# A linear-attention decoder layer: where the transposes of the key-value sums stand among the projections

## The chip, the cores and the metric

The kernel runs on one core of one Trainium2 chip. The metric is device time in microseconds (us), the median of the runs. An engine takes its own instructions in the order in which they are written; engines meet only through semaphores. PE is TensorE, DVE is VectorE, ACT is ScalarE, POOL is GpSimd, SP issues most of the transfers.

## What is computed

A decoder layer on x of 8 batches x 1024 rows x 512 columns, in three parts, each followed by a layer norm of x plus the part's result:

```
q, k, v = x @ Wq.T + bq, x @ Wk.T + bk, x @ Wv.T + bv     # 16 heads of 32
q', k'  = [cos(p), sin(p)] / sqrt(128),  p = head @ proj / sqrt(32)   # 128 cosines, 128 sines
kv      = sum over the rows of k'^T v      # per batch and head, 256 x 32
x = layernorm(x + (q' kv) @ Wo.T + bo)
x = layernorm(x + rmsnorm(x) @ W_in.T + b_in + row of a decayed context table)
x = layernorm(x + dequant(fp6(x)) @ dequant(fp6(Wf)).T + bias)
```

The change concerns the attention alone: the sums `kv` can be used by the query side only once they are complete, and they have to be transposed on the way.

## The kernel before

**Two stages.** `attention` handles the first line-up (q, k, v, features, kv, output projection, first norm) and writes `normed`; `context_and_quantised` does the other two parts. The first ends at about 1290 us of the span, the second takes the rest. Only the first is changed.

**Batches and chunks.** A batch has two chunks of 512 rows. The engines run batch 0 in mode "first", batches 1 to 7 as one loop body (mode "loop"), and then what is left over as "tail". Work is split into steps, and all engines walk through the same list of steps (lines 112 to 158), each taking its own share of each step. The list is written out by hand in 16 slots, numbered by feature pair w: pairs 0 to 7 are keys, 8 to 15 queries.

**The steps.** K(c, g) and Q(c, g) project chunk c for four heads (group g): 12 matmuls of 512 columns into one PSUM bank, then ACT adds the bias and writes `stack_hi`, and DVE writes the rest, `stack_lo` (line 726), which frees the bank. V(c, t) and W(c, t) (the step "wo") are tiles of 12 matmuls as well: V gives values, W the output projection, which DVE adds to `res` (line 753) and takes statistics of (line 756). phase(w) multiplies by `proj` into four banks of their own; ACT rounds the result (line 610), DVE subtracts (line 713), ACT takes the sine (line 617), DVE the magnitude (line 720), ACT the cosine (line 623). kv(w) adds one key pair into `kv_sum` (32 matmuls, line 530), and out(w) multiplies one query pair by `kv_cols` (16 matmuls, line 556) into the same PSUM, after which ACT and DVE write `att_hi` and `att_lo` (lines 635, 747). W(1, t) within a loop body belongs to the batch before.

**The sums.** save(0) and save(1) ("kvsave", DVE, line 737) copy two groups of `kv_sum` each to `kv_rows`, once kv(5) and kv(7) are done. turned(0) and turned(1) ("kvt") transpose them: PE does four 128x128 transposes into a bank (line 543), DVE copies that to `kv_cols` (line 740). out(8) needs turned(0), out(9) needs turned(1).

**The two banks.** All steps in `GEMM` (K, Q, V, W and kvt) share two PSUM banks in turn, in the order of the list: the n-th takes bank n % 2. Before PE writes one, it waits until DVE has read what the step two places earlier in that list left there:

```
GEMM = ("k", "q", "v", "wo", "kvt")
b = bank[order.ring(mode, s, 2)]
freed(n - 2)        # pe.wait_ge(bank_free, ...)
```

The place of a kvt step in the list thus sets the bank, and the predecessor waited for, of every tile near it. In slots 8 and 9 the list of these steps reads: Q(0,2), turned(0), W(1,1), Q(0,3), turned(1), W(1,2). In mode "first" there are no W(1, t), since they belong to the batch before, and in the tail there is no kvt.

**Beside it.** POOL splits the transposed x of the next chunk into high and low parts (lines 371, 375), one such split once Q(0,3) is done, and computes the norm's factors (lines 397 to 404) once stats(1) in slot 10 is done. Those belong to no slot of the change.

Of the kernel before, what the change touches and what calls it, by code (L numbers as in the profile page):

```python
# [98 lines left out]
def attention_steps():  # L99

    K = lambda c, g: ("k", c, g)
    Q = lambda c, g: ("q", c, g)
    V = lambda c, t: ("v", c, t)
    W = lambda c, t: ("wo", c, t)
    kv = lambda w: ("kv", w)
    out = lambda w: ("out", w)
    sin = lambda w: ("sin", w)
    cos = lambda w: ("cos", w)
    wf = lambda n: ("wf", n)
    save, turned = (lambda n: ("kvsave", n)), (lambda n: ("kvt", n))  # L110
    stats, norm = (lambda c: ("stats", c)), (lambda c, h: ("norm", c, h))
    after = {
        11: [sin(11), Q(1, 1), cos(11), norm(1, 0), norm(1, 1), V(0, 0), out(10)],
        12: [sin(12), Q(1, 2), cos(12), V(0, 1), out(11)],
        13: [sin(13), Q(1, 3), cos(13), W(0, 0), W(0, 1), out(12)],
        14: [sin(14), K(0, 0), cos(14), W(0, 2), W(0, 3), stats(0), out(13)],
        15: [sin(15), K(0, 1), cos(15), V(0, 2), norm(0, 0), out(14), norm(0, 1)],
        0: [sin(0), K(0, 2), cos(0), V(0, 3), out(15)],
        1: [sin(1), K(0, 3), cos(1), V(1, 0), kv(0)],
        2: [sin(2), K(1, 0), cos(2), V(1, 1), kv(1)],  # L120
        3: [sin(3), K(1, 1), cos(3), kv(2)],
        4: [sin(4), K(1, 2), cos(4), V(1, 2), kv(3)],
        5: [sin(5), K(1, 3), cos(5), V(1, 3), kv(4)],
        6: [sin(6), Q(0, 0), cos(6), kv(5)],
        7: [sin(7), Q(0, 1), cos(7), save(0), W(1, 0), kv(6)],
        8: [sin(8), Q(0, 2), cos(8), turned(0), W(1, 1), kv(7), save(1)],
        9: [sin(9), Q(0, 3), turned(1), cos(9), W(1, 2), out(8)],
        10: [sin(10), Q(1, 0), cos(10), W(1, 3), stats(1), out(9)],
    }
    steps = []  # L130
    for w in range(PAIRS_A):
        steps += [("phase", w)] + after[w]
    turn = steps.index(V(0, 0))
    own = {K(0, 0), K(0, 1)} | {V(0, t) for t in range(TPC)}
    left = {x for x in steps[turn:] if x not in own} | {out(15), stats(1)} | {norm(1, h) for h in range(2)} | {W(1, t) for t in range(TPC)}
    steps = steps[turn:] + steps[:turn]

    after = {
        0: [K(0, 1), sin(0), K(0, 2), cos(0), V(0, 0), V(0, 1)],
        1: [sin(1), K(0, 3), cos(1), V(0, 2), V(0, 3), V(1, 0), kv(0)],  # L140
        2: [sin(2), K(1, 0), cos(2), V(1, 1), kv(1)],
    }
    first = [K(0, 0)]
    for w in range(3):
        first += [("phase", w)] + after[w]
    first += [x for x in steps[steps.index(("phase", 3)):] if x not in left]

    after = {
        12: [sin(12), Q(1, 2), wf(0), cos(12), wf(1), out(11)],
        13: [sin(13), Q(1, 3), cos(13), wf(2), W(0, 0), W(0, 1), out(12)],  # L150
        14: [sin(14), cos(14), W(0, 2), W(0, 3), stats(0), out(13)],
        15: [sin(15), cos(15), wf(3), out(14), wf(4), norm(0, 0), norm(0, 1), out(15), wf(5), W(1, 0), W(1, 1), ("ends",), W(1, 2), ("repeats",), W(1, 3),
             stats(1), norm(1, 0), norm(1, 1)],
    }
    tail = [("win",), out(10)]
    for w in range(START + 1, PAIRS_A):
        tail += [("phase", w)] + after[w]
    return steps, left, tail, first


def attention(nc, x, xT, WqT, bq, WkT, bk, WvT, bv, WoT, bo, proj, eye, lens, triangle, WinT, g_res, Wf,
              b_in, g_init, decay, places, ctx_in, kept, normed):

    steps, left, tail, first = attention_steps()
    assert {s for s in steps if s not in left} == set(first)
    GEMM = ("k", "q", "v", "wo", "kvt")
# [1171 lines left out]
```

## Time and profile before

| | us |
|---|---|
| median of 3 runs (1793.45 to 1803.18) | 1795.09 |
| the profiled execution's own time | 1793.82 |
| its span | 1792.0 |
| PE busy | 1635.3 (91%) |
| DVE busy | 1210.9 (68%) |
| ACT busy | 1152.0 (64%) |
| POOL busy | 690.9 (39%) |

Busy times are sums over the span. A row of the timeline gives the start, the duration, the engine, the line, the operation and its tiles, how many such instructions follow one another, and in brackets how long the engine had been idle before it and what ended that. The ends of matmuls are modelled; the starts are not, so distances between starts are what to reckon with. "PEclk" is TensorE's granted clock as a share of 2.4 GHz.

### The profile page before, as it was taken

Reading aid. Unit: us, or ns where it says so; the run is one execution under the profiler, and the core shown is the slowest. Engines: PE = TensorE matmul, PEld = TensorE weight load, DVE = VectorE, ACT = ScalarE, POOL = GpSimd, SP = SyncE. Lnnn points to the kernel's source line nnn. Section 1 sums busy time; section 2 is a strip of 40 time slices with the busy share of each in tenths; the row PEclk is TensorE's granted clock in tenths of the full one; section 3 lists DMA queues with packets and bytes.
Section 4 is the critical chain, followed back from the end, with each engine's and each line's share of the span. In section 5 each row is a group of like instructions: output and inputs, shape, how many; then the busy total and the mean of one; then the engine's idle time right before and its main releaser. Section 6 shows DMA issues by size and latency. Waiting matters only on the chain. (4 is left out here: it accounts for less than half of the span.)

```text
span 1792.0 us, 31892 instructions
## 1 busy us (share of the span) xinstructions
PE 1635.3 (91%) x12212; PEld 1169.2 (65%) x12212; DVE 1210.9 (68%) x1815; ACT 1152.0 (64%) x1510; POOL 690.9 (39%) x641
## 2 busy tenths in 40 slices
PE   4999989998998999999899999987489999999996
PEld 3756766675675666567567656754358777787784
DVE  4577666666765766665676667569767777777774
ACT  2687776776676778667677776766136555565564
POOL 3033105203411420340242044004448777877786
PEclk9999999999999999999999999999789999999998
DMA  4100202200210220120022022001331222222201
GB/s 157 49 21 4 72 1 72 71 1 9 81 54 1 72 72 1 35 88 22 1 72 71 1 72 71 25 1 47 99 104 51 86 77 77 88 70 77 71 36 59
DMA packets 49102, 95.87 MB, mean 54 GB/s; under 512 B 3472, under 2 KB 3792, under 8 KB 48976
## 3 DMA queue, kind: packets, MB, share of 16 engines
q1 hardware_dynamic: 38864, 76.29, 13.6%
q10 hardware_dynamic: 10112, 17.69, 2.7%
q8 instruction: 105, 1.72, 0.4%
q14 instruction: 21, 0.17, 0.0%
HBM read 60.38 MB, written 33.59 MB: 52 GB/s over the span
## 5 line engine op out<-in xcount | busy, mean ns | idle before, releaser
L713 DVE SCALAR_TENSOR_TENSOR feat<-feat,phases 128x1024 f32<-128x1024 f32 x256 | 301.1, 1218 | 209.8 <-ACT feat L610 209.7
L610 ACT ACTIVATE feat<-phases 128x1024 f32<-128x1024 f32 x256 | 248.6, 1024 | 157.7 <-PE phases L469 95.3
L617 ACT ACTIVATE feat<-feat 128x1024 f32<-128x1024 f32 x256 | 272.0, 1063 | 60.6 <-DVE feat L713 52.0
L371 POOL TENSOR_TENSOR xt_hi<-xt_raw,zero 128x512 fp32r<-128x512 f32 x60 | 72.3, 1235 | 534.8 <-PE bank L460 525.9
L623 ACT ACTIVATE feat<-feat 128x1024 f32<-128x1024 f32 x256 | 256.7, 1048 | 12.4 <-DVE feat L720 12.3
L720 DVE TENSOR_SCALAR feat<-feat 128x1024 int32<-128x1024 int32 x256 | 204.0, 799 | 48.2 <-ACT feat L617 47.9
L384 POOL TENSOR_TENSOR res<-res,bo_all 128x512 f32<-128x512 f32 x64 | 78.0, 1243 | 180.0 <-DMA res<-x 179.8
L556 PE MATMUL kv_sum<-feat,kv_cols 128*32 128x512 f32 x1024 | 126.6, 613 | 8.3 <-ACT feat L623 8.3
L530 PE MATMUL kv_sum<-feat,v 128*32 128x256 f32 x2048 | 124.1, 383 | 7.8 <-DVE v L733 7.8
L458 PE MATMUL bank<-xt_hi,win_hi 128*128 128x512 f32 x256 | 109.3, 427 | 19.4 <-POOL xt_lo L375 19.4
L1073 PE MATMUL bank<-wf_hi,back_hi 128*128 128x512 f32 x256 | 109.2, 427 | 3.5 <-DVE back_lo L1211 3.5
L458 PE MATMUL bank<-xt_hi,wq_hi 128*128 128x512 f32 x256 | 107.9, 422 | 3.8 <-DVE stack_lo L726 3.8
L1173 ACT ACTIVATE xs<-xs,shift,rstd 128x512 f32<-128x512 f32 x96 | 71.6, 809 | 60.2 <-POOL shift L1048 60.2
L458 PE MATMUL bank<-wo_hi,att_hi 128*128 128x512 f32 x224 | 97.4, 435 | 13.1 <-DVE stack_lo L726 8.1
L1073 PE MATMUL bank<-win_hi,turn_hi 128*128 128x512 f32 x256 | 104.4, 408 | 2.1 <-DVE turn_lo L1211 2.0
L458 PE MATMUL bank<-wf_hi,xt_hi 128*128 128x512 f32 x256 | 101.3, 396 | 3.7 <-DVE wf_lo L666 2.3
L1075 PE MATMUL bank<-wf_hi,back_lo 128*128 128x512 f32 x256 | 103.9, 406 | 0.0
L1074 PE MATMUL bank<-wf_lo,back_hi 128*128 128x512 f32 x256 | 103.8, 405 | 0.0
L530 PEld LDWEIGHTS kv_sum<-feat,v 128*32 128x32 f32 x2048 | 60.2, 110 | 64.7 <-issue 20.9
L459 PE MATMUL bank<-xt_lo,win_hi 128*128 128x512 f32 x256 | 101.9, 398 | 0.0
L460 PE MATMUL bank<-xt_hi,win_lo 128*128 128x512 f32 x256 | 101.8, 398 | 0.0
L753 DVE TENSOR_TENSOR res<-bank,res 128x512 f32<-128x512 f32 x64 | 43.9, 686 | 85.4 <-PE bank L460 81.3
(196 smaller groups left out, 4088.6 us busy)
## 6 DMA issues: line engine op xcount, KB each, us to landing
normed<-res SPq DMA_DIRECT2D x32, 513.0 KB, 4.5
xt_raw<-xT SPq DMA_DIRECT2D x16, 1024.0 KB, 6.5
res<-x SPq DMA_DIRECT2D x32, 512.0 KB, 4.3
xs<-normed SPq DMA_DIRECT2D x24, 513.0 KB, 4.0
out<-xs ACTq DMA_DIRECT2D x24, 512.0 KB, 2.8
feat<-normed SPq DMA_DIRECT2D x8, 513.0 KB, 3.8
out<-feat ACTq DMA_DIRECT2D x8, 512.0 KB, 2.8
xt_raw<-ctx SPq DMA_DIRECT2D x8, 256.0 KB, 3.7
```

What stands on the lines that cost most here:

```text
L458: pe.matmul(out, left_hi(n), right_hi(n), start=(n == 0), stop=False)
L459: pe.matmul(out, left_hi(n), right_lo(n), start=False, stop=False)
L530: last = pe.matmul(kv_sum[DH * h:DH * h + DH, g, :], v[c][:, t, col:col + DH], feat[2 * (w % 2) + h // 2][:, :, at:at + MAP],  start=(c == ...
L556: last = pe.matmul(b[DH * h:DH * h + DH, :], kv_cols[:, half, g * P + h * DH:g * P + h * DH + DH], feat[2 * (w % 2) + h // 2][:, half, (h ...
L610: act.activation(feat[2 * (w % 2) + p][:, 0, :], phases[:, 2 * p:2 * p + 2, :].rearrange("p h n -> p (h n)"), ACT.Identity, bias=ROUND).th ...
L617: act.activation(f[:, 1, :], f[:, 0, :], ACT.Sin, scale=-TWO_PI).then_inc(sin_done, 1)
L623: act.activation(f[:, 0, :], f[:, 0, :], ACT.Sin, scale=-TWO_PI, bias=HALF_PI).then_inc(feat_ready, 1)
L713: dve.scalar_tensor_tensor(f[:, 0, :], f[:, 0, :], ROUND, phases[:, 2 * p:2 * p + 2, :].rearrange("p h n -> p (h n)"), ALU.subtract, ALU.s ...
L720: dve.tensor_scalar(f[:, 0, :].bitcast(I32), f[:, 0, :].bitcast(I32), MAGNITUDE, None, ALU.bitwise_and).then_inc(fold_ready, 1)
L1073: pe.matmul(o, hi[:, cols], w_hi[:, n, :], start=(n == 0), stop=False)
L1074: pe.matmul(o, hi[:, cols], w_lo[:, n, :], start=False, stop=False)
L1075: last = pe.matmul(o, lo[:, cols], w_hi[:, n, :], start=False, stop=(closed and n == KD - 1))
```

## The change

turned(0) moves in slot 8 from ahead of W(1,1) to behind kv(7), and turned(1) in slot 9 from ahead of cos(9) to behind out(8). Nothing else is edited; banks and waits follow from the list.

```
-        8: [sin(8), Q(0, 2), cos(8), turned(0), W(1, 1), kv(7), save(1)],
-        9: [sin(9), Q(0, 3), turned(1), cos(9), W(1, 2), out(8)],
+        8: [sin(8), Q(0, 2), cos(8), W(1, 1), kv(7), turned(0), save(1)],
+        9: [sin(9), Q(0, 3), cos(9), W(1, 2), out(8), turned(1)],
```

The list of the steps that share the two banks becomes: Q(0,2), W(1,1), turned(0), Q(0,3), W(1,2), turned(1).

## Rows read from the trace of the kernel before

**Rows 1.** The page: busy per engine, and granted clock in 40 slices of the span.
```profile
PE 1635.3 (91%) x12212; PEld 1169.2 (65%) x12212; DVE 1210.9 (68%) x1815; ACT 1152.0 (64%) x1510; POOL 690.9 (39%) x641
...
PEclk9999999999999999999999999999789999999998
```

**Rows 2.** Waits of PE, 0 to 1300 us: total us, times, longest.
```profile
PE bank L458 <- DVE stack_lo L726: 54.4, 33, 3.4
```

**Rows 3.** Timeline of PE, slots 7 to 10 of batch 3.
```profile
551.97 0.39 PE L458 MATMUL bank<-wo_hi,fold 128*128 128x512 f32 x1
...
554.83 1.93 PE L530 MATMUL kv_sum<-feat,v 128*32 128x256 f32 x32
556.69 0.51 PE L476 MATMUL phases<-stack_hi,proj_hi 32*128 32x512 f32 x4
...
557.60 0.50 PE L458 MATMUL bank<-xt_hi,wq_hi 128*128 128x512 f32 x1
...
560.50 0.60 PE L543 MATMUL bank<-ident,kv_rows 128*128 128x128 f32 x4
563.73 0.60 PE L458 MATMUL bank<-wo_hi,fold 128*128 128x512 f32 x1 [2.63 <-DVE stack_lo L726]
...
570.13 0.51 PE L476 MATMUL phases<-stack_hi,proj_hi 32*128 32x512 f32 x4
...
577.93 0.79 PE L458 MATMUL bank<-wo_hi,fold 128*128 128x512 f32 x1 [3.39 <-DVE stack_lo L726]
...
582.31 1.92 PE L556 MATMUL kv_sum<-feat,kv_cols 128*32 128x512 f32 x16
584.16 0.50 PE L476 MATMUL phases<-stack_hi,proj_hi 32*128 32x512 f32 x4
```

**Rows 4.** Stretches of batch 3: busy per engine, then PEclk, DMA share, GB/s.
```profile
552.00:557.00 5.00, 5.00 (x49) 3.28 (x51) 4.53 (x8) 4.59 (x5) 0.00 (x0) 1.00 0.00 0
...
564.00:567.40 3.40, 3.40 (x9) 2.61 (x9) 0.28 (x1) 0.76 (x1) 0.00 (x0) 0.50 0.03 5
```

**Rows 5.** Timeline of PE, batch 0: the longer of its two waits in slots 9 and 10.
```profile
124.91 0.50 PE L458 MATMUL bank<-xt_hi,wq_hi 128*128 128x512 f32 x1 [1.70 <-DVE stack_lo L726]
```

**Rows 6.** Timeline of PE, batch 7: starts of phases 8, 9 and 10.
```profile
1172.08 0.51 PE L476 MATMUL phases<-stack_hi,proj_hi 32*128 32x512 f32 x4
...
1183.96 0.51 PE L476 MATMUL phases<-stack_hi,proj_hi 32*128 32x512 f32 x4
...
1197.41 0.50 PE L476 MATMUL phases<-stack_hi,proj_hi 32*128 32x512 f32 x4
```

**Rows 7.** Timeline of DVE, slots 7 and 8 of batch 3.
```profile
556.20 0.68 DVE L753 TENSOR_TENSOR res<-bank,res 128x512 f32<-128x512 f32 x1
...
562.93 0.74 DVE L726 SCALAR_TENSOR_TENSOR stack_lo<-bank,bq_col,stack_hi 128x512 fp32r<-128x512 f32 x1
563.59 0.68 DVE L740 COPY kv_cols<-bank 128x512 f32<-128x512 f32 x1
...
572.29 2.35 DVE L713 SCALAR_TENSOR_TENSOR feat<-feat,phases 128x1024 f32<-128x1024 f32 x2 [1.33 <-ACT feat L610]
```

**Rows 8.** Timeline of ACT, slots 9 and 10 of batch 3.
```profile
571.23 1.95 ACT L610 ACTIVATE feat<-phases 128x1024 f32<-128x1024 f32 x2 [6.47 <-PE phases L476]
...
576.21 2.10 ACT L623 ACTIVATE feat<-feat 128x1024 f32<-128x1024 f32 x2
```

**Rows 9.** Timeline of POOL, batch 3: the split, then the norm's factors.
```profile
574.18 4.93 POOL L371 TENSOR_TENSOR xt_hi<-xt_raw,zero 128x512 fp32r<-128x512 f32 x4 [70.46 <-PE bank L460]
579.19 5.00 POOL L375 TENSOR_TENSOR xt_lo<-xt_raw,xt_hi 128x512 fp32r<-128x512 f32 x4
```

**Rows 10.** Timeline of DVE, batch 0: two magnitudes beside POOL's split.
```profile
129.07 3.40 DVE L720 TENSOR_SCALAR feat<-feat 128x1024 int32<-128x1024 int32 x2
```

**Rows 11.** Timeline and stretch, PE at slot 13 of batch 2.
```profile
463.62 0.50 PE L458 MATMUL bank<-wo_hi,att_hi 128*128 128x512 f32 x1 [1.42 <-DVE stack_lo L726]
...
463.60:467.00 3.40, 3.38 (x16) 2.33 (x20) 1.57 (x3) 0.40 (x1) 3.32 (x4) 1.00 0.00 0
```

## The prediction, made before the changed kernel was run

> **What bounds the kernel now.** I read the page first: TensorE is busy for 1635.3 of 1792.0 us, far ahead of DVE, ACT and POOL, and its clock is nearly full everywhere [rows 1]. So the questions are where TensorE stands still and where it runs slowly. The view of its waits answers the first for the attention stage (0 to 1300 us): 54.4 us in 33 waits all have one form, a projection tile whose bank waits for DVE's `stack_lo`; the longest is 3.4 us [rows 2].
>
> The timeline of one batch shows where they lie [rows 3]. In slot 8 the transposes start at 560.50 and are modelled to end at 561.10; then TensorE is idle for 2.63 us, and W(1,1) starts at 563.73. In slot 9 the idle time ahead of W(1,2) is 3.39 us. These two make 6.02 us a batch. The cause can be read from the list of bank users: W(1,1) stands two places behind Q(0,2), so it waits until ACT and DVE have read Q(0,2)'s bank. DVE's `stack_lo` runs from 562.93 to 563.67 [rows 7], and W(1,1) starts 0.06 us after it. Between Q(0,2) and W(1,1) TensorE has only 0.60 us of transposes. ACT and DVE are no faster because they are still busy with the sine and the magnitude of pair 8, which their queues hold ahead of it.
>
> There is a second cost behind the idle time. From 564.00 to 567.40 the granted clock is 0.50, that is 1.2 GHz, against 1.00 (2.4 GHz) in the stretch before [rows 4]. W(1,1) then takes far longer than its like: W(1,0), at full clock, goes from 551.97 to the next start at 554.83, 2.86 us. In total, phase 8 to phase 9 is 570.13 - 556.69 = 13.44 us, and phase 9 to phase 10 is 584.16 - 570.13 = 14.03 us [rows 3].
>
> **What the moves do.** No instruction is added or taken away: 4 transposes and one DVE copy per kvt, twice a batch, stand elsewhere. No DMA and no ACT instruction belongs to them, and no step of SP's or POOL's is passed.
>
> *Slot 8.* W(1,1) now stands two places behind W(1,0), whose bank DVE reads from 556.20 to 556.88 [rows 7]. Q(0,2) ends its issue at 560.50, so W(1,1) need not wait. The slot is then a plain sum of starts: phase 557.60 - 556.69 = 0.91, Q 560.50 - 557.60 = 2.90, W 2.86, kv(7) like kv(6) 556.69 - 554.83 = 1.86, transposes 0.60 (the modelled length of four; a bit long). Sum 9.13 us. Gain 13.44 - 9.13 = 4.31 us: 2.63 idle and the rest clock.
>
> *turned(0) itself.* It now waits for Q(0,2)'s `stack_lo`, the wait that W(1,1) had. It comes to its turn at 556.69 + 9.13 - 0.60 = 565.22, and `stack_lo` is there at 563.67: 1.55 us spare, because W(1,1) and kv(7), 4.72 us, now lie between.
>
> *Slot 9.* Phase 9 starts at 565.82 instead of 570.13. Q(0,3) needs the bank of W(1,1), whose issue ended at 563.36. DVE reads it right behind `stack_lo`, some 0.7 us, so by about 564.4; Q(0,3) starts at 566.73. W(1,2) needs turned(0)'s bank: its copy, 0.68 us [rows 7], follows the transposes and is over by 566.6, and W(1,2) starts at 569.63. The slot is 0.91 + 2.90 + 2.86 + out(8) 584.16 - 582.31 = 1.85 + 0.60 = 9.12 us, a gain of 14.03 - 9.12 = 4.91 us. turned(1) waits for Q(0,3)'s `stack_lo`. The rounding of pair 8 would start at about 566.9 (phase start plus 571.23 - 570.13 = 1.10 [rows 3, 8]). From there a chain of ACT and DVE leads to `stack_lo`, which in slot 9 must end before its cosines do, about 578.31 - 571.23 = 7.1 us later [rows 8]; turned(1) comes up at about 574.3. So at worst, with 574.0, it just fits. This is the tightest place. out(8) needs turned(0)'s copy (566.6, against 572.5): covered. Slot 10's W(1,3) needs turned(1)'s copy, due about 576.4 against 578.6: covered. out(9) comes still later.
>
> *What is queued behind the moved steps.* On DVE save(1) stands behind turned(0)'s copy, and the subtraction of phase 9 behind both. Subtractions begin 572.29 - 571.23 = 1.06 us after ACT's rounding begins [rows 7, 8], here about 568.0; copy and save, 1.4 us, end by about 567.3. In slot 10 the copy of turned(1) stands behind out(8)'s `att_lo` and ahead of the subtraction of phase 10. I see a free space of about 0.6 us for its 0.68, and take nothing. Bounds for the DVE side per batch: 0, or both copies in full, 2 x 0.68 = 1.4 us. Near nothing is the better value, since ACT stands still for 6.47 us ahead of its rounding now [rows 8], and after the change its chain of 7.1 us still has to fit only a slot of 9.1.
>
> *POOL.* Its split starts with Q(0,3)'s end, so it moves ahead by the 4.3 us of slot 8, while slot 10's work moves ahead by 9.2. It lasts from 574.18 to 584.19 [rows 9] and now reaches into slot 10, where before it ended ahead of that slot's rounding. Rows of batch 0 show what such an overlap can cost: two magnitudes took 3.40 us beside the split [rows 10]. Slot 10 has room for it. I take 0; the bounds are 0 and 1 us a batch. The Trainium skill, "SBUF — State Buffer", section "Who interferes with whom", says the same in general: VectorE and GpSimd share one port pair, and whoever comes first blocks the other for a whole instruction. That rule alone would give a price for each magnitude and would not change the sum here, as long as the slot is TensorE's.
>
> *The clock.* If the idle time goes, does the clock stay up? Batch 0 has a wait of 1.70 us in slot 10 [rows 5] and batch 2 one of 1.42 us in slot 13, and behind the latter the stretch reads 1.00 [rows 11]. What would be left in slots 8 and 9 is nothing. I take the full clock.
>
> **The sum.** Batches 1 to 6 have the pattern of batch 3: 6 x (4.31 + 4.91) = 55.3 us. In batch 7 the distances are 1183.96 - 1172.08 = 11.88 (the clock stayed up in its slot 8) and 1197.41 - 1183.96 = 13.45 [rows 6]: 2.75 + 4.33 = 7.1 us. Batch 0 has no W(1, t): its bank users follow in the same order as before, Q(0,2), turned(0), Q(0,3), turned(1), so its waits stay, and a copy ahead of phase 10's subtraction could cost up to 0.7. I take 0. The second stage starts earlier and is otherwise the same; a clock step that falls elsewhere may be worth 1 or 2 us either way (one such half-rate stretch cost at most 4.91 - 3.39 = 1.5 us here). Total 62.4 us. The profiled execution took 1793.82 us, so 1731.4; the median of the runs is 1.27 us above it, so about 1732 to 1733. I say 1732. Its own range is 1726 to 1742, from the bounds above (8 batches x 1.0 to 1.4 us on the late side; transposes whose modelled 0.60 is too long, 14 of them, and the clock steps on the early side).
>
> **Rivals.**
>
> *Half a gain: the clock goes on falling.* For it: the price of the slow stretches is a third of my sum. The mechanism would be that the small waits left in each batch, 1.42 us at slot 13 being one, pull the clock down instead. Then only the idle time comes back: 6 x 6.02 and, if batch 7's two waits are each like slot 8's 2.63, 5.3 more = 41.4 us, 1754 us. Against it: the stretch behind that very wait ran at 1.00 [rows 11]. In the Trainium skill, "TensorE: Matmul & The Clock Gate", section "A second HAM failure mode: psum-queue depth-cycling", frequent short idle times between groups that take turns in PSUM banks are said to make the clock oscillate. By that rule this rival would come true, since the two banks still take turns; the trace so far speaks against it. Chance 0.07.
>
> *Half a gain: turned(1) is late.* If Q(0,3)'s `stack_lo` is put off by one more magnitude beside POOL's split (half of 3.40 = 1.7 us [rows 10]) from the 574.0 above, TensorE waits 1.4 us for it, and 7 batches lose 10 us: 1742. This lies in the range, and I count it with the forecast.
>
> *No change: the wait only moves.* TensorE would wait as long ahead of Q(0,3) for DVE's reading of W(1,1), or in turned(0). For it: all of this still hangs on the same DVE queue. Against it: the spare times above, 1.5 and 2.3 us in slot 8. Time 1795. Chance 0.03.
>
> *Slower: DVE's queue becomes the bound.* In slots 8 and 9 the copies now stand directly ahead of the next pair's subtraction, on which sine, magnitude and cosine hang. If that chain set the slots, the stalls would stay, in new places, and 2 x 0.68 us a batch would come on top: 8 x 1.4 = 11 us, 1806. It decides from the point at which the chain of 7.1 us plus a copy is longer than TensorE's slot of 9.1. The rows say 7.8. Chance 0.04.
>
> The forecast gets 0.86. The range for 8 times in 10 is 1725 to 1743. What a measurement can tell from no change is about 0.5%, 9 us: faster 0.93, same 0.03, slower 0.04.
>
> **What would show it.** In the trace after: the projection tiles of slots 8 and 9 without an idle time; the total of the `stack_lo` waits down from 54.4 to about 13 us; phases 8, 9 and 10 each 9.1 us apart; no granted clock of 0.50 between batch 1 and batch 7's slot 9. I am wrong if TensorE shows a wait ahead of turned(0), Q(0,3) or turned(1) of over 1 us, if half-rate stretches appear elsewhere in the batch, or if slot 10 grows beyond the sum of its starts, 0.91 + 2.90 + 2.86 + 1.85 = 8.5 us, which would be the DVE queue or POOL.

## The result and the profile after

The changed kernel takes 1734.43 us (1732.11 to 1734.57, 4 runs) against 1796.76 us (1793.45 to 1803.18, 4 runs) for the kernel before: ratio 0.9645, 95% interval 0.9627 to 0.9664. The forecast was 1732, range 1725 to 1743. The profiled execution took 1734.53 us, with a span of 1732.7.

The page of the changed kernel, busy times and granted clock in 40 slices, against [rows 1]:

```profile
PE 1616.4 (93%) x12212; PEld 1158.9 (67%) x12212; DVE 1212.9 (70%) x1815; ACT 1150.7 (66%) x1510; POOL 689.0 (40%) x641
...
PEclk9999999999999999999999999997799999999998
```

The same instructions run; TensorE is busy for 19 us less: the stretches with a granted clock of 0.50 add up to 90 us of the span instead of 128, and half of those 38 us is 19. The other 40 us of the difference in span are idle time.

The waits of PE, 0 to 1300 us, against [rows 2]; the columns are total us, times, longest:

```profile
PE bank L458 <- DVE stack_lo L726: 16.1, 19, 2.3
```

54.4 us in 33 waits became 16.1 in 19: the 14 waits ahead of W(1,1) and W(1,2) are gone, and one new size stands out, 2.3 us in slot 0 of batch 0, ahead of any step that was moved.

Slots 8, 9 and 10 of batch 3 in the timeline of PE, against [rows 3], and the stretch around them, against [rows 4]:

```profile
541.16 0.51 PE L476 MATMUL phases<-stack_hi,proj_hi 32*128 32x512 f32 x4
...
550.27 0.51 PE L476 MATMUL phases<-stack_hi,proj_hi 32*128 32x512 f32 x4
...
558.78 0.66 PE L543 MATMUL bank<-ident,kv_rows 128*128 128x128 f32 x4
559.36 0.51 PE L476 MATMUL phases<-stack_hi,proj_hi 32*128 32x512 f32 x4
...
567.88 0.51 PE L476 MATMUL phases<-stack_hi,proj_hi 32*128 32x512 f32 x4
```

```profile
541.00:568.00 27.00, 27.00 (x190) 17.54 (x188) 22.64 (x32) 20.51 (x23) 9.99 (x8) 1.00 0.01 1
```

Phases 8, 9, 10 and 11 start 9.11, 9.09 and 8.52 us apart. No row between them carries an idle time, TensorE is busy for 27.00 of 27.00 us, and the granted clock is 1.00 throughout.

DVE in the same slots, against [rows 7]:

```profile
552.42 2.35 DVE L713 SCALAR_TENSOR_TENSOR feat<-feat,phases 128x1024 f32<-128x1024 f32 x2 [0.76 <-ACT feat L610]
554.77 2.57 DVE L720 TENSOR_SCALAR feat<-feat 128x1024 int32<-128x1024 int32 x2
557.27 0.74 DVE L726 SCALAR_TENSOR_TENSOR stack_lo<-bank,bq_col,stack_hi 128x512 fp32r<-128x512 f32 x1
```

The copy of turned(0) (from 550.37) and save(1) (from 550.98, 0.68 us) end 0.76 us before the subtraction of phase 9 can begin. `stack_lo` of Q(0,3) ends at 558.01, and turned(1), which waits for it, starts at 558.78: 0.77 us spare, the tightest place. Beside POOL's split the two magnitudes take 2.57 us, as long as in the kernel before.

Summed over batches 1 to 7 (distances between starts of phases), slots 8 and 9 fell from 190.8 to 127.5 us, a gain of 63.3. Slot 13 grew by 3.1 us and slot 11 by 0.5. Batch 0 took 3.0 us more in its slot 0, ahead of any step that was moved; the executions below show 19.4, 21.0 or 22.4 us there. The sum of any other slot is within 0.9 us of before.

### The profile page after: what moved, and what is told of

It is laid out like the page before. It is cut to its first block and busy times, and to the rows that moved or that the text cites. A ratio compares the mean times of both kernels' runs of the same rounds, so it can differ in the third digit from the quotient of the medians.

```text
span 1732.7 us, 31892 instructions
## 1 busy us (share of the span) xinstructions
PE 1616.4 (93%) x12212; PEld 1158.9 (67%) x12212; DVE 1212.9 (70%) x1815; ACT 1150.7 (66%) x1510; POOL 689.0 (40%) x641
## 5 line engine op out<-in xcount | busy, mean ns | idle before, releaser
L623 ACT ACTIVATE feat<-feat 128x1024 f32<-128x1024 f32 x256 | 256.8, 1047 | 11.2 <-DVE feat L720 11.0
L458 PE MATMUL bank<-wo_hi,att_hi 128*128 128x512 f32 x224 | 90.8, 405 | 13.6 <-DVE stack_lo L726 9.9
L459 PE MATMUL bank<-xt_lo,wq_hi 128*128 128x512 f32 x256 | 101.9, 398 | 0.0
```

Source lines behind the costliest of these rows:

```text
L458: pe.matmul(out, left_hi(n), right_hi(n), start=(n == 0), stop=False)
L459: pe.matmul(out, left_hi(n), right_lo(n), start=False, stop=False)
L623: act.activation(f[:, 0, :], f[:, 0, :], ACT.Sin, scale=-TWO_PI, bias=HALF_PI).then_inc(feat_ready, 1)
```

## The experiments

The times of the kernel before are the medians of its runs beside each group: 1798.54 us for the first four, 1801.45 us for the next four, and a single run of 1798.68 us for the last. The changed kernel was timed beside 1796.76 us, so kernels of different groups are compared by their ratios as well.

**One move alone, slot 8.**

```
-        8: [..., cos(8), turned(0), W(1, 1), kv(7), save(1)],
+        8: [..., cos(8), W(1, 1), kv(7), turned(0), save(1)],
```

> Only turned(0) is moved behind kv(7); slot 9 keeps turned(1) ahead of W(1,2). Theory (each projection tile waits for the bank left two places earlier, so each move removes its own slot's wait, clock loss included): slot 8 falls from 13.44 to 9.11 us in batches 1 to 6 and from 11.88 to 9.11 in batch 7; slot 9 keeps an idle time of 2.64 us ahead of W(1,2) and comes to 13.44, since the slow W(1,1) no longer lengthens it from 3.39. Sum 6 x (4.33 + 0.7) + 2.8 = 33 us, about 1762. Rival (the clock loss needs both waits close together): slot 9 runs at full clock, 11.9 us, and the gain is 43 us, about 1752.

Measured 1770.22 us, ratio 0.9834 (0.9806 to 0.9862): 28 us by the medians, less than the theory (1762 us) and the rival (1752 us) had. Slot 8 is 9.11 us in all seven batches, as both said. Slot 9 is between 14.15 and 15.17 us in batches 1 to 6, longer than either theory had it; only in batch 7 does it run at full clock (11.86 us). Its row and its stretch in batch 1:

```profile
265.45 0.80 PE L458 MATMUL bank<-wo_hi,fold 128*128 128x512 f32 x1 [3.39 <-DVE stack_lo L726]
```

```profile
264.50:271.00 6.50, 5.55 (x16) 3.94 (x20) 1.49 (x3) 1.33 (x2) 6.42 (x6) 0.50 0.00 0
```

The idle time stays at 3.39 us although W(1,1) ran at full clock, so my reason for the step from 2.64 to 3.39 was wrong (the last experiment takes this up). And the half-rate stretch is twice as long here as in [rows 4], 6.8 us against 3.4; that is so in batches 1, 2, 4 and 5, while in batches 3 and 6 it is 3.4 us. The moves do work one by one. The rival in which the clock falls only if both waits are close together is refuted: one wait alone pulls the clock down.

**One move alone, slot 9.**

```
-        9: [sin(9), Q(0, 3), turned(1), cos(9), W(1, 2), out(8)],
+        9: [sin(9), Q(0, 3), cos(9), W(1, 2), out(8), turned(1)],
```

> Only turned(1) is moved behind out(8); slot 8 keeps turned(0) ahead of W(1,1). Theory: slot 9 falls from 14.1 to 9.10 us in batches 1 to 6 and from 13.45 to 9.10 in batch 7, slot 8 keeps 2.63 us idle and 13.44 us: 6 x 5.0 + 4.35 = 34.5 us, about 1761. The two single moves then sum to about 4 us more than both together. Rival (the clock loss needs both waits close together): slot 8 at 11.9 us, gain 44 us, about 1751.

Measured 1755.99 us, ratio 0.9755 (0.9728 to 0.9782): 43 us by the medians. Slot 9 is 9.1 us in all batches. Slot 8 keeps its idle time everywhere, but is 13.4 us in batches 1, 4, 6 and 7, and 11.9 in batches 2, 3 and 5. In one of the latter:

```profile
406.66 0.50 PE L458 MATMUL bank<-wo_hi,fold 128*128 128x512 f32 x1 [2.65 <-DVE stack_lo L726]
```

```profile
399.00:412.00 13.00, 10.35 (x96) 6.90 (x88) 8.26 (x12) 7.22 (x8) 0.00 (x0) 1.00 0.00 1
```

So the same wait of 2.65 us is followed by half rate in some batches and not in others. What removing a wait of this length is worth is not fixed: 2.8 us (11.87 - 9.11) or 4.3 us (13.44 - 9.11). Neither theory had that, and a time between their two follows from it.

**The idle time filled, nothing moved.**

```
+                        for again in range(5):
                         for half in range(2): ...
                             last = pe.transpose(b[:, to:to + P], ...)
```

> The order of before, but TensorE does each set of four transposes five times over (16 redundant transposes more per kvt), which fills most of the idle time with work; bank waits stand where they stood. Theory (a large part of the gain is the clock that falls behind the idle time): idle ahead of W(1,1) and W(1,2) shrinks to some 0.3 to 0.6 us, W(1,1) still starts at the same moment, but at full clock: slots 8 and 9 come to 11.9 us each instead of 13.44 and 14.1. 6 x (1.56 + 2.25) + 1.6 = 24 us, about 1771, no stretch at half clock in slots 8 and 9. Rival (the slow stretches belong to these slots for another reason, the transposes among them): no gain or slower, 1795 or above.

Measured 1774.43 us, ratio 0.9876 (0.9841 to 0.9912): 24 us by the medians, 22 by the ratio. The row of W(1,2) in batch 3, and a stretch that holds slots 8 and 9:

```profile
569.07 0.51 PE L458 MATMUL bank<-wo_hi,fold 128*128 128x512 f32 x1 [1.65 <-DVE stack_lo L727]
```

```profile
549.00:575.00 26.00, 23.45 (x185) 16.24 (x174) 16.23 (x20) 14.30 (x17) 9.60 (x8) 1.00 0.01 1
```

TensorE does 16 more transposes per kvt and the kernel is faster, because the granted clock stays at 1.00: slot 8 is 11.87 us in every batch instead of 13.44, slot 9 is 12.61 instead of 14.1. W(1,2) starts 4.0 us behind the first transpose in both kernels (0.60 + 3.39 us before, 2.35 + 1.65 here), so nothing but the rate of the work behind it has changed. That is 6 x (1.57 + 1.5) + 1.6 = 20 us of the 63: a third of the change's gain is clock, two thirds idle time. Twenty transposes took 2.35 us, 0.12 each, so the fill was smaller than I had reckoned, and 0.90 us in slot 8 and 1.65 us in slot 9 stayed idle.

**Another predecessor, the same moment.**

```
+        8: [sin(8), turned(0), Q(0, 2), cos(8), W(1, 1), kv(7), save(1)],
+        9: [sin(9), turned(1), Q(0, 3), cos(9), W(1, 2), out(8)],
```

> turned(0) and turned(1) stand behind sin(w) and ahead of Q(0,2) and Q(0,3). W(1,1) and W(1,2) no longer wait for the stack_lo of the projection ahead of them, but for DVE's copy of the transposes, which DVE makes behind the magnitudes, at about the moment at which stack_lo is made today. Theory (what counts is when DVE gets to the read, not whose bank it is): the waits stay at 2.5 to 2.7 us, only their releaser is now the copy; within 5 us of before. Rival (it was the neighbourhood of the projection and its stack_lo alone): the waits are gone and the time is about 1735.

Measured 1799.84 us, ratio 1.0 (0.9976 to 1.0023): no change. The row of W(1,1) in batch 4:

```profile
717.73 0.51 PE L458 MATMUL bank<-wo_hi,fold 128*128 128x512 f32 x1 [2.63 <-DVE kv_cols L740]
```

W(1,1) waits 2.63 us as before, for another instruction in the same place of DVE's queue: the copy runs from 716.99, right behind the second magnitude of pair 8. W(1,2) waits 3.77 us, a little longer than the 3.39 of before. Which step stands two places ahead does not decide it alone; it matters when DVE comes to the read.

**The same, ahead of the sine.**

```
+        8: [turned(0), sin(8), Q(0, 2), cos(8), W(1, 1), kv(7), save(1)],
+        9: [turned(1), sin(9), Q(0, 3), cos(9), W(1, 2), out(8)],
```

> turned(0) and turned(1) stand first behind the phase, ahead of sin(w). DVE's copy then comes ahead of the magnitudes. Theory (when DVE gets to the read decides): the copy follows the second subtraction and ends about 5.1 to 5.8 us behind the phase's start, while W(1,1) comes up 0.91 + 0.53 + 2.90 = 4.3 us behind it: 0.8 to 1.4 us idle remain per slot, no clock loss: slots of 9.9 to 10.5, that is 11 to 19 us above the changed kernel: 1746 to 1754. Rival (any place ahead of W(1,t) costs the full wait): about 1795.

Measured 1745.68 us, ratio 0.9696 (0.9667 to 0.9724). DVE copies ahead of its magnitudes (from 693.53; the magnitudes begin at 694.13), and W(1,1) waits 0.80 us, without half rate behind it:

```profile
694.27 0.50 PE L458 MATMUL bank<-wo_hi,fold 128*128 128x512 f32 x1 [0.80 <-DVE kv_cols L740]
```

Slots 8 and 9 take 9.98 to 9.99 us, 0.88 above those of the change; 14 x 0.88 = 12 us should separate the two kernels; it is 11 us by the medians and 9 by the ratios (0.9696 and 0.9645).

**DVE's copy three times over, on the changed kernel.**

```
+                        for again in range(2):
+                            dve.tensor_copy(kv_cols..., b...).then_inc(copied, 1)
+                            dve.wait_ge(copied, 4 * i + 2 * s[1] + again + 1)
```

> The changed kernel with each DVE copy to kv_cols made three times, one behind the other with a semaphore between (1.5 to 2 us more of DVE per kvt, 16 times). Theory (slots 8 and 9 are TensorE's with spare time on the ACT and DVE chain): the subtractions of pairs 9 and 10 come some 1 us later, the chain of 7.1 us still fits the slot of 9.1; nothing waits longer than 0.5 us: 1734 to 1740. Rival (the DVE queue is next in line): all of it shows, 14 x 1.5 = 21 us or more, 1755.

Measured 1735.32 us, ratio 0.9641 (0.9608 to 0.9674), the same as the change within the intervals. One of PE's waits, 180 to 1150 us:

```profile
PE bank L544 <- DVE stack_lo L727: 1.3, 6, 0.2
```

Slot 9 grows from 9.10 to 9.38 us in batches 1 to 6, and what waits there is turned(1), for 0.2 us: the place named as the tightest. DVE's queue is not the next bound in slot 8, and in slot 9 it is reached only with two more copies.

**out(12) between the two tiles of slot 13, on the changed kernel.**

```
-        13: [sin(13), Q(1, 3), cos(13), W(0, 0), W(0, 1), out(12)],
+        13: [sin(13), Q(1, 3), cos(13), W(0, 0), out(12), W(0, 1)],
```

> The changed kernel with out(12) put between W(0,0) and W(0,1) in slot 13 of the loop, so that 1.9 us of TensorE work lie between Q(1,3) plus W(0,0) and the tile that waits for Q(1,3)'s stack_lo. Theory: the wait of 1.07 to 1.31 us ahead of W(0,1) goes in 7 batches: 7 to 8 us less, about 1727. Rival (the wait comes back behind, in slot 14 or in out(12) that waits for its features): the same as the changed kernel.

Measured 1727.38 us, ratio 0.9594 (0.9569 to 0.9619). Slot 13 comes to 11.48 us in batches 1 to 6, where the changed kernel has 12.6 to 12.9, and to 11.47 in batch 0 (12.62); slots 14 and 15 stay at 11.8 and 8.4. PE's waits, 180 to 1150 us, first a row of the changed kernel, then two of this one:

```profile
PE bank L458 <- DVE stack_lo L726: 8.6, 12, 1.3
```

```profile
PE kv_sum L530 <- DVE v L733: 6.8, 7, 1.0
PE bank L458 <- DVE stack_lo L726: 1.7, 6, 0.3
```

**And V(1,3) ahead of K(1,3).**

```
-        5: [sin(5), K(1, 3), cos(5), V(1, 3), kv(4)],
+        5: [sin(5), V(1, 3), K(1, 3), cos(5), kv(4)],
```

> The changed kernel with out(12) between W(0,0) and W(0,1), and V(1,3) ahead of K(1,3) in slot 5, so that kv(4) no longer waits 0.97 us for DVE's reading of V(1,3). Theory: 7.5 us from slot 13 and 8 x 0.97 = 7.8 us from slot 5: about 1719. Rival (the later key product delays the cosines of pair 5, and slots 6 and 7, which are short on TensorE, wait for ACT): slot 5 gains and slots 6 and 7 give it back, 1727 or more.

Measured 1722.53 us (1717.53 to 1730.62, 6 runs), ratio 0.956 (0.9535 to 0.9584), the lowest median of all versions. The interval of its ratio lies clear of the change's, but not clear of that of the kernel with out(12) alone. Slot 5 is 9.44 us instead of 10.10, slots 6 and 7 stay at 6.35 and 9.12, and among PE's waits from 180 to 1150 us is this row:

```profile
PE kv_sum L530 <- DVE v L733: 2.2, 7, 0.3
```

At most 0.3 us of the wait of 0.97 remains, and 8 x 0.66 = 5 us came back and not the 7.8 of the theory.

**POOL's split behind the norm's factors, on the filler kernel.**

```
-                if mode != "last":
-                    split(i + 1, 0, i, mode)
                 powers(2 * i - 1)
+                if mode != "last":
+                    split(i + 1, 0, i, mode)
```

> The filler kernel (order of before, transposes five times over), with POOL's split of the next chunk put behind powers(2i-1), so that it no longer runs beside slot 9's magnitudes. The question: why slot 9's idle time is 3.39 us in batches 1 to 6 and 2.64 in batch 7. Theory (POOL's split holds up DVE's magnitudes, 2.57 us for two against 1.83): slot 9 falls from 12.61 to 11.87 us in batches 1 to 6 as well. Rival (it comes from the slot ahead, W(1,1) or TensorE's own work): slot 9 stays at 12.61 us. The end may shift by what the later split costs elsewhere; only slot 9 is read.

A single run, on another chip, took 1857.09 us; it is read for slot 9 alone. The rows of W(1,2) and of V(0,0) in batch 3:

```profile
594.14 0.50 PE L458 MATMUL bank<-wo_hi,fold 128*128 128x512 f32 x1 [0.90 <-DVE stack_lo L727]
...
622.65 0.79 PE L458 MATMUL bank<-wf_hi,xt_hi 128*128 128x512 f32 x1 [11.23 <-POOL xt_lo L375]
```

Slot 9 is 11.85 to 11.89 us in batches 1 to 6, and its two magnitudes, which beside the split take 2.57 us together, take 0.69 us each and end 1.82 us after the first begins. The theory holds: the longer wait of slot 9 is DVE's magnitudes held up by POOL. The second row is the price that the expectation left open: V(0,0) in slot 11 is the first user of the split, and with the split this late it waits 11.2 us in each of six batches, with 10 to 14 us at 1.2 GHz around it, so that slot 11 grows by 13 us.

## Why the prediction was right, step by step

*The slots.* The sums of starts gave 9.13 and 9.12 us; measured are 9.11 and 9.10. The gain in them was forecast as 62.4 us and is 63.3. Each single move brought its own slot to that length. One name in the working is wrong and none of its numbers: the rounding that starts 1.10 us behind phase 9 is that of pair 9, not of pair 8.

*The cause.* The first reading, that W(1,1) waits for the bank of Q(0,2), was right but not complete. The pair of kernels with the transposes placed early shows that a bank with another reader does not help (1799.84 us) as long as DVE's magnitudes stand ahead of that reader, and helps (1745.68 us) once they stand behind it. What the change does is to let W(1,1) and W(1,2) follow tiles whose banks DVE has long read, while the steps that need the late read of `stack_lo`, turned(0) and turned(1), have a projection tile and a product ahead of them as cover, 4.7 us in the trace (W(1,1) starts at 544.96, turned(0) at 549.68).

*The clock.* A third of the forecast sum was clock, 62.4 less the 41.4 of idle time, and the filler kernel confirms its size, 20 us by its slots. The rival in which the clock goes on falling is refuted for this kernel: waits of 1.31 us in slot 13 and 0.97 in slot 5 remain in the changed kernel, and no stretch at 1.2 GHz lies between batch 0 and the tail. The Trainium skill, "TensorE: Matmul & The Clock Gate", section "A second HAM failure mode: psum-queue depth-cycling", has the clock oscillate when matmul groups that cycle through PSUM banks idle often and briefly; it names no length of the idle times. The traces do not agree for short waits. Over all eleven traces, from slot 1 of batch 0 to slot 10 of batch 7, this is how often the granted clock read 0.50 within a wait of PE or in the 3 us behind it:

| idle time of PE, us | how many | with 0.50 |
|---|---|---|
| 0.97 to 1.44 | 130 | 0 |
| 1.54 to 1.70 | 15 | 1 |
| 2.57 to 2.65 | 24 | 17 |
| 3.39 and above | 24 | 24 |

The one case in the second row is the wait of 1.56 us in slot 10 of batch 0 of the kernel with both more moves. So the forecast was right to price the waits of 2.6 and 3.4 us with clock and those left without, but the rows that it had for the latter, one stretch at full clock behind a wait of 1.42 us, were few.

*The tight place.* I had turned(1) fit with 0.3 us to spare; it had 0.77, and three copies instead of one used that up. The rival "turned(1) is late" did not come true, and the rival "DVE's queue becomes the bound" did not either: two more copies a time cost 1 us in all by the medians and nothing by the ratios.

*What was off.* The remaining `stack_lo` waits were to total about 13 us and are 16.1. Of the difference, 1.9 us lie ahead of W(0,1) in slot 13 of batches 1 to 6, and 1.6 us in slot 0 of batch 0, where a wait of 0.72 us became 2.31. In slot 13 of batch 3 the two magnitudes take 2.90 us beside POOL's adds and split (before they were 0.70 and 1.01 us long, and 2.14 us from the start of the first to the end of the second).

```profile
589.71 2.90 DVE L720 TENSOR_SCALAR feat<-feat 128x1024 int32<-128x1024 int32 x2
```

I had taken POOL's cost as 0 where the split meets slots 9 and 10, and that was right there, but I did not look at slot 13, where POOL's next adds and split fall against the same magnitudes. In both traces these start when a transfer lands, in batch 3 about 0.6 us earlier within the slot than before; why was not tried. Nor is it sure that the change does this: the wait in slot 13 was 0.56 us in four batches and 1.4 in two in the kernel before, and in the kernel with three copies, where TensorE has the same order, slot 13 is 0.7 us longer over batches 1 to 6 and not 1.8. The other 1.3 of the 3.1 us by which slot 13 grew are in batch 7, where it belongs to the tail and has 10.2 us at 1.2 GHz instead of 3.4.

The span fell by 59.3 us: 63.3 in slots 8 and 9, less 3.1 in slot 13, 0.5 in slot 11 and 3.0 in batch 0's first slot, and 2.6 more over all the rest. The sum of the forecast had none of these last four, and they scatter from execution to execution by about as much. So the mechanism was forecast, but that the median came within 2.4 us of 1732 is in part luck. In the expectation for the first single move I also put the difference between the waits of 2.64 and 3.39 us down to the slow W(1,1); the last experiment shows POOL's split in its place.

## What to carry to other kernels

When few banks are used in turn, look for each tile that waits for a bank at the queue of the engine that reads it. Order the steps so that the next tile takes a bank that was read long ago, and so that a step which needs a late read comes behind other work. Price an idle time of TensorE with the slower matmuls behind it, but from several repetitions, since the same wait may or may not bring them. Before a step on a shared helper engine is moved later, find its first user.

## What was not expected of the hardware

The same wait of 2.65 us was followed by half rate in four of seven batches and not in three, within one execution. Behind a wait of 3.39 us the clock stayed at 1.2 GHz for 3.4 us in every batch of the kernel before, and for 3.4 or 6.8 us in the kernel with only turned(0) moved. Redundant transposes made a kernel 24 us faster by the medians.

The second stage, in which these kernels do not differ, took a different time from one profiled execution to another: from its first count matmul to the end 488.6 us in the changed kernel, and 497.0 in the kernel with both more moves. Busy times of the engines in that stretch (PE, PEld, DVE, ACT, POOL), then PEclk:

```profile
1244.10:1732.70 488.60, 455.52 (x2140) 364.07 (x2140) 349.43 (x687) 267.77 (x536) 364.80 (x316) 0.96 0.22 72
```

```profile
1231.80:1728.80 497.00, 464.08 (x2140) 369.20 (x2140) 349.73 (x687) 267.80 (x536) 364.66 (x316) 0.94 0.21 70
```

The traces say where the 8.4 us are. TensorE runs the same 2140 matmuls and is busy for 8.6 us more, while DVE, ACT and POOL are busy for the same time to 0.3 us. The granted clock is 0.50 for 31.9 us of the stretch in the one and 49.3 us in the other, 17.4 us more, and half of that is 8.7. The kernel with only turned(0) moved shows the same longer second stage (497.0 us, of which 49.3 at 0.50). So a stage that no edit touched can differ by 8 us by TensorE's clock alone; what makes the clock take one course or the other was not tried. That is more than the moves in slots 5 and 13 bring each, so those are judged by the lengths of their slots and by the medians of five and six runs, and not by the span of one execution.
